# Staging the edge keys of a graph-layer count build on GpSimd instead of VectorE

## What is computed

```python
x = x + gnn(layernorm(x), stack([src, dst]), edge_attr, ...)
x = x + ffn(layernorm(x), ...)

def gnn(x, edge_index, edge_attr, ...):
    row, col = edge_index
    deg = segment_sum(ones, col);  dinv = where(deg > 0, deg ** -0.5, 0)
    norm = dinv[row] * dinv[col]
    for l in range(5):
        edge_fea = concatenate([edge_attr[:, 3:] @ ew1[l], edge_attr[:, 0:3] @ ew2[l]])
        msg = norm[:, None] * (h[row] + edge_fea)
        agg = segment_sum(msg, col)
        h = relu(concatenate([h, agg]) @ mlp_w[l] + mlp_b[l])
        h = batchnorm(h)            # relu too, but for the last layer
    return h
```

## Time and profile before

| | |
|---|---|
| median of three runs | 1666.47 us (1665.78 to 1670.65) |
| the profiled execution | 1666.33 us, its span 1664.6 us |
| TensorE (PE) busy | 1444.7 us, 87% |
| VectorE (DVE) busy | 705.1 us, 42% |
| ScalarE (ACT) busy | 389.3 us, 23% |
| GpSimd (POOL) busy | 165.3 us, 10% |
| one-hots cnt (L1521), x63 | 75.1 us, 1193 ns each |
| one-hots ohS (L1523), x504 | 117.6 us busy, 306 ns each |
| even and odd fields (L1625) | 93 and 61 instructions up to 440 us |

### The profile page before, as it was taken

One profiled execution on the slowest core, in us unless ns is written; L12 is line 12 of the kernel. 1 busy time (PEld: TensorE's weight loads), 2 busy tenths in 40 slices (PEclk: granted clock), 3 DMA queues, 4 the chain that ended last, 5 costly groups with the idle time before them and its releaser, 6 DMA issues.

```text
span 1664.6 us, 25197 instructions
## 1 busy us (share of the span) xinstructions
PE 1444.7 (87%) x8538; PEld 808.6 (49%) x8539; DVE 705.1 (42%) x1938; ACT 389.3 (23%) x1010; POOL 165.3 (10%) x145
## 2 busy tenths in 40 slices
PE   2565689889888999989999899989999863999996
PEld 2554444444443544445454444535444433666664
DVE  6989999999522220123001220122201356233332
ACT  1320444444302400032001310014000330333332
POOL 1000000000000000000000000000000004466663
PEclk9865799999999999989999999999999876999999
DMA  5153000000000000000000000000005090333333
GB/s 136 39 183 125 2 1 1 2 1 2 14 1 13 1 1 1 0 15 1 1 1 0 14 1 1 1 1 13 1 1 103 5 347 13 54 65 63 63 63 41
DMA packets 49551, 57.88 MB, mean 35 GB/s; under 512 B 14319, under 2 KB 41601, under 8 KB 49184
## 3 DMA queue, kind: packets, MB, share of 16 engines
q1 hardware_dynamic: 38688, 41.67, 8.7%
q0 software_dynamic: 10752, 14.69, 5.5%
HBM read 42.36 MB, written 13.99 MB: 34 GB/s over the span
## 4 chain that ended last, share of the span: by engine, by line
PE 79%; DVE 13%; issue 3%; DVEq 2%; ACT 1%; DMA 1%; POOL 1%; SPq 0%; POOLq 0%
PE bank L654 40%; PE bank L735 13%; PE bank L1148 6%; PE bank L1163 6%; PE bank L1752 3%; DVE ohS L1523 2%; PE bank L1697 2%; PE bank L1154 1%; PE bank L644 1%; DVE ohL L1409 1%; PE bank L738 1%; PE bank L1750 1%; PE bank L1140 1%; DVEq L505 1%; PE bank L1114 1%
## 5 line engine op out<-in xcount | busy, mean ns | idle before, releaser
L654 PE MATMUL bank<-at,m 125*128 125x500 fp8e4 (+1 forms) x3500 | 697.9, 356 | 10.4 <-issue 5.3
L654 PEld LDWEIGHTS bank<-at,m 125*128 125x128 f16 x3500 | 318.3, 98 | 342.8 <-issue 35.9
L663 DVE TENSOR_TENSOR aggT<-bank,dinvB 128x500 f32<-128x500 f32 (+1 forms) x70 | 42.3, 621 | 353.0 <-PE bank L654 352.8
L826 ACT ACTIVATE hT<-bank,prm 128x500 f32<-128x500 f32 (+1 forms) x70 | 40.5, 630 | 601.2 <-PE bank L738 601.2
L874 POOL TENSOR_TENSOR idJ<-idJ,wts 125x1400 f32<-125x1400 f32 x2 | 8.0, 4006 | 1380.6 <-DVE idJ L1032 1380.6
L788 DVE BATCH_NORM_STATS2 zst<-hT 128x6 f32<-128x500 f32 (+1 forms) x70 | 40.3, 617 | 198.4 <-ACT hT L826 198.4
L735 PE MATMUL bank<-hT,wcur 128*128 128x500 f32 (+1 forms) x280 | 124.2, 566 | 0.0
L1523 DVE TENSOR_SCALAR ohS<-iotaS,now 128x128 bf16<-128x128 bf16 x504 | 117.6, 306 | 0.0
L735 PE MATMUL bank<-aggT,wcur 128*128 128x500 f32 (+1 forms) x280 | 116.4, 538 | 0.0
L623 DVE SCALAR_TENSOR_TENSOR m<-bank,dinvP,m 125x256 f16<-125x256 f32 x100 | 48.0, 483 | 145.7 <-ACT m L635 145.7
L1148 PE MATMUL bank<-w1s,xtT 128*128 x224 | 107.7, 603 | 0.3 <-issue 0.2
(11 more groups left out here) (318 smaller groups left out, 1325.7 us busy)
## 6 DMA issues: line engine op xcount, KB each, us to landing
slrow<-sl_dram SPq DMA_DIRECT2D x26, 512.0 KB, 5.0
w1s<-in_L_ffn_W SPq DMA_DIRECT2D x1, 4096.0 KB, 14.5
w2s<-in_L_ffn_W SPq DMA_DIRECT2D x1, 4096.0 KB, 19.0
xin<-in_x SPq DMA_DIRECT2D x1, 2800.0 KB
x<-in_x SPq DMA_DIRECT2D x1, 2800.0 KB
out_rows<-x SPq DMA_DIRECT2D x1, 2800.0 KB
xn_dram<-xn SPq DMA_DIRECT2D x1, 2800.0 KB
wraw<-in_L_gnn_mlp_w SPq DMA_DIRECT2D x5, 512.0 KB, 3.7
```

Of the source, the lines that this page charges most:

```text
L654: last = pe.matmul(bank[banks[g % len(banks)]][:, 0:w], m[:, s, k, h * 128:(h + 1) * 128], at_block(g // H)[:, s, :], start=s == 0 and k = ...
```

## The change

GpSimd gets the staging of each strip (`stage`) and the odd fields (`high_nibbles`); VectorE keeps the one-hots and the even fields. GpSimd copies the keys first into a new buffer `rawKD` and waits for that copy (`s_raw`) before it subtracts the strip's offset. The odd fields are no longer shifted and masked: `encI - encB` leaves them four bits up, and ScalarE scales by 1/16 as it writes them. `s_nib` becomes `s_low` (VectorE) and `s_high` (GpSimd). The low nibbles, the one-hots and the order of VectorE's other steps stay.

```diff
+        def stage(pool, w):
+            side = w % 2
+            first, mine, past = first_chunk(pool, w), turns(pool, w), turns_before(pool, w)
+            with pool.Fori(0, mine) as i:
+                c = chunk_of(first, i)
+                pool.wait_ge(s_free[side], past + i + 1)
+                pool.tensor_copy(now[:, side, :, :], tab[:, :, bass.ds(c, U)])
+                pool.tensor_copy(rawKD[:, side, :, :], kd[:, :, bass.ds(c, U)]).then_inc(s_raw[side], 1)
+                pool.wait_ge(s_raw[side], past + i + 1)
+                pool.sem_inc(s_apart, 1)
+                pool.tensor_scalar(nowKD[:, side, :, :], rawKD[:, side, :, :], float(-W * w), None, ALU.add).then_inc(s_now[side], 1)
+
+        def high_nibbles(pool, u):
+            pool.wait_ge(s_low, u + 1)
+            pool.tensor_tensor(encI[:, u % 2, :], encI[:, u % 2, :], encB[:, :], ALU.subtract).then_inc(s_high, 1)
...
+            pool.wait_ge(s_rng, 1)
+            pool.wait_ge(s_ez, 1)
+            for w in range(NW):
+                stage(pool, w)
+                if w % 2 and w > 1:
+                    high_nibbles(pool, w // 2 - 1)
+            for u in range(PAIRS - 2, PAIRS):
+                high_nibbles(pool, u)
             gather_pool(pool)
...
-                dve.tensor_scalar(encB[:, :], encI[:, u % 2, :], NIBBLES, None, ALU.bitwise_and).then_inc(s_nib, 1)
-
-            def high_nibbles(u):
-                dve.wait_ge(s_nib, 2 * u + 1)
-                dve.tensor_scalar(encI[:, u % 2, :], encI[:, u % 2, :], 4, NIBBLES, ALU.logical_shift_right, ALU.bitwise_and).then_inc(s_nib, 1)
+                dve.tensor_scalar(encB[:, :], encI[:, u % 2, :], NIBBLES, None, ALU.bitwise_and).then_inc(s_low, 1)
...
-            ahead = first_chunk(dve, 0), turns(dve, 0), turns_before(dve, 0)
+            ahead = turns(dve, 0), turns_before(dve, 0)
...
                 with dve.Fori(0, mine) as i:
-                    c = chunk_of(first, i)
-                    dve.wait_ge(s_free[side], past + i + 1)
-                    dve.tensor_copy(now[:, side, :, :], tab[:, :, bass.ds(c, U)])
-                    dve.tensor_scalar(nowKD[:, side, :, :], kd[:, :, bass.ds(c, U)], float(-W * w), None, ALU.add).then_inc(s_now[side], 1)
                     dve.wait_ge(s_now[side], past + i + 1)
...
                 if side and w > 1:
                     low_nibbles(w // 2 - 1)
-                    high_nibbles(w // 2 - 1)
...
-                    act.wait_ge(s_nib, 2 * u + 1 + odd)
+                    act.wait_ge(s_high if odd else s_low, u + 1)
...
-                                              byte[:, f, :, 0:n], ACT.Copy, saturate=False,
+                                              byte[:, f, :, 0:n], ACT.Copy, scale=1.0 / 16 if odd else 1.0, saturate=False,
```

More of the change, by code:

```diff
@@ L147, in gnn_ffn_program @@
         nowKD = r("nowKD", [128, 2, 2, U], I16)
+        rawKD = r("rawKD", [128, 2, 2, U], I16)
         now = r("now", [128, 2, ROWS, U], BF16)
@@ L362, in gnn_ffn_program @@
         s_now = [sem(f"s_now{r}") for r in range(2)]
+        s_raw = [sem(f"s_raw{r}") for r in range(2)]
         s_oh = [sem(f"s_oh{r}") for r in range(2)]
@@ L366, in gnn_ffn_program @@
         s_enc = sem("s_enc")
-        s_nib = sem("s_nib")
+        s_low = sem("s_low")
+        s_high = sem("s_high")
         s_xf = sem("s_xf")
@@ L1509, in _ @@
             evicted = 0
-            ahead = first_chunk(dve, 0), turns(dve, 0), turns_before(dve, 0)
+            ahead = turns(dve, 0), turns_before(dve, 0)
             for w in range(NW):
                 side = w % 2
-                first, mine, past = ahead
+                mine, past = ahead
                 with dve.Fori(0, mine) as i:
-                    c = chunk_of(first, i)
-                    dve.wait_ge(s_free[side], past + i + 1)
-                    dve.tensor_copy(now[:, side, :, :], tab[:, :, bass.ds(c, U)])
-                    dve.tensor_scalar(nowKD[:, side, :, :], kd[:, :, bass.ds(c, U)], float(-W * w), None, ALU.add).then_inc(s_now[side], 1)
                     dve.wait_ge(s_now[side], past + i + 1)
@@ L1525, in _ @@
                 if w + 1 < NW:
-                    ahead = first_chunk(dve, w + 1), turns(dve, w + 1), turns_before(dve, w + 1)
+                    ahead = turns(dve, w + 1), turns_before(dve, w + 1)
                 if side and w > 1:
                     low_nibbles(w // 2 - 1)
-                    high_nibbles(w // 2 - 1)
                 if w > SB and w % SB == 3:
@@ L1539, in _ @@
                 low_nibbles(u)
-                high_nibbles(u)
             attribute_sums(NQ - 2)
```

## The result

The changed kernel takes 1709.32 us, the median of four runs (1707.82 to 1711.44), against 1667.43 us for the kernel before, measured beside it. The ratio is 1.025, with a 95% interval of 1.0228 to 1.0271: 2.5% slower. The forecast was 1716 us. The profiled execution took 1710.67 us, 44.3 more than the profiled one of before.

What follows compares the result with a forecast made beforehand. Count build paced by VectorE first, later by VectorE and TensorE nearly equally; turns 200.3, chains 99.6, gaps 12.8, evictions 4.8 sum to 317.5 us, last strip 49.3 us later; 1666.3 + 49.3 gives 1716 us, range 1683 to 1750.

Steps and rivals of the forecast that it cites:

- The sign: Whole kernel: slower than before, chance 0.92; same 0.05, faster 0.03.
- The chain, 2.88 us: From VectorE's low nibbles to the next ohD, after strips 3, 5, ... 61: VectorE waits 2.88 us for GpSimd's staging, 30 times.
- The subtraction hidden under the loads: GpSimd's 125x500 subtraction, about 0.9 us, lies beside 2.05 us of register loads and set-up, so costs nothing.
- the dearer rival: GpSimd's small operations stand behind long VectorE ones (19 us more), or the subtraction blocks register loads (27 more): 1735 to 1745 us; chance 0.15.
- The queue stands on its wait: GpSimd's queue does not run past an unmet wait, so three register loads, 1.65 us, come after it in each chain.
- the rival of 1684 us: GpSimd's queue runs ahead of its wait, register loads done meanwhile; chain 1.83 us, 31.5 us less; chance 0.17.
- 32 gaps of 0.40 us: At the other strip starts, GpSimd's copy and add exclude VectorE or wait for it: 0.40 us each, 12.8 us in all.
- The loop's end: What follows the count build loop needs the last dense groups as before and doesn't change; it shifts whole.
- The clock: Rival: TensorE idles more and runs at the lower clock; 0 to 8 us allowed, inside the range, no separate chance.
- TensorE covers it: Rival: from strip 13 on TensorE hides a chain of up to 1.25 us; about 1667 us; not slower or faster, chance 0.08.
- The rule on exclusion: Skill's statement that GpSimd and two-input VectorE operations exclude each other; the rows agree, the sum would be no other.

Runs made afterwards that it cites:

- e4: Changed kernel with GpSimd loading the next strip's three registers before it waits for the even fields; 1688.09 us, ratio 1.0107 to the kernel before.
- e1: Changed kernel with high_nibbles of a pair run after the staging of the next even strip instead of before it; 1670.73 us, ratio 1.0015 to the kernel before.
- e3: VectorE stages as in the kernel before, GpSimd does only the odd fields by the subtraction; 1673.41 us, ratio 1.0021 to the kernel before.
- e6: e3 with GpSimd's subtraction held until VectorE has done cnt of the next strip; 1673.69 us, ratio 1.0021 to the kernel before.
- e2: Changed kernel with only the staging on GpSimd, VectorE doing both nibbles by masks; 1663.18 us, ratio 0.9965 to the kernel before.

## Why the prediction was right, and where it was off

The sign, the mechanism and the place are as forecast: VectorE idles in front of ohD after each odd strip from 3 on and not after even ones, released by GpSimd, and everything behind the loop moves as a whole.

- *The chain, 2.88 us.* Measured 2.96 at 293.51. Its parts: loads and set-up from 290.60 to the copy at 292.61, 2.01 (forecast 2.05); copy 0.28 (0.28), behind whose first 0.22 us a second copy starts, rawKD, which the sum had forgotten; from its start to the add 0.40, and the add 0.25. The forecast of 0.25 + 0.15 for wait and add was too little, and the second copy was missing, but it had allowed up to 0.7 here. The mean over the 30 chains is 3.01 us, since in a few GpSimd's queue stood 0.3 us longer between two steps (3.30 us for the chain after strip 7); why, the record doesn't show. The attribute sums hid under the chain, as forecast. From first to last ohD the strips take 305.1 us; 62 turns of 3.18 and 8 evictions of 0.6 leave 103 us for the chains with their even fields, for which the sum had 99.6.
- *The subtraction hidden under the loads.* True: it ends at 291.89, the copy starts at 292.61. Its length was mis-sized, 1.25 instead of 0.9 us, inside the bound of 1.4, and it would have shown only from 2.05 on. e4 makes it visible. That it would keep the queue from loading registers, the other half of the dearer rival, is out as well: the first load starts at 290.60 and the subtraction at 290.64, side by side.
- *The queue stands on its wait.* This step carried the forecast against the rival of 1684 us. The 4.32 us without a queue operation, and the first load at 290.60, show it in this kernel, and in all 30 chains the first load starts 0.04 us before the subtraction; the trace has the wait on the subtraction itself, not on an instruction of its own; e4, which does by hand what the rival assumed, takes 1688 us. The measurement differs here from the Trainium skill (Perfetto Trace Analysis, Per-engine timelines), by which the sequencer is free again once the instruction is in the wait queue.
- *32 gaps of 0.40 us.* This is the term that failed: 12.8 us that aren't there. The gap after even strips is 0.00, but for one of 0.35 us between the second and third strip. The reasoning from the earlier trace rows took exclusion as a toll on each of GpSimd's operations. It is one, but it depends on what is met. GpSimd's small copies come 1.8 us into the turn, when VectorE is at its short ohS, and slip in; the longest ohS of the changed kernel took 0.41 us instead of 0.31, and the turn is 3.18 us all the same. With the chains, 3 us more than summed, that puts the last ohD at 473.2 instead of 482.3, 9 us early. The total is only 7 us under the forecast, since the part behind the loop, put at no change, got 4 us longer in the profiled execution: that much of the closeness is luck.
- *The loop's end.* The forecast called what follows the loop unchanged. About half a microsecond of the 4 is a second meeting with the subtraction. VectorE's multiplication in the last attribute sums, 0.17 us before, reads in the order of time:

```profile
482.19 1.24 POOL L539 TENSOR_TENSOR encI<-encI,encB 125x500 int32<-125x500 int32 x1 [4.04 <-DVE encB L1515]
...
482.26 1.20 DVE L1528 TENSOR_TENSOR s4P<-s4P,dinvP 125x16 f32<-125x16 f32 x1
```

  It happens in all six attribute sums that meet a subtraction. The 1.03 us is partly paid for by the odd fields that VectorE no longer does: from the last count products to the next dense product it is 8.15 us, 7.58 before.
- *The clock.* The forecast allowed 0 to 8 us. In the dense stretch the mean granted clock fell from 1.00 to 0.93, and between 168 us and the last count products TensorE was at its lower level, 1.2 GHz, for 72 us instead of 38. The ohD dates above add up without it, so inside the build it cost next to nothing: the 0.35 us gap, where GpSimd's copy waited for count products of 1.85 us. Behind the loop it was at the lower level for 124 us, 110 before. Over the traces of all eight kernels, that part goes from 1227 us with 110 us at the lower level to 1236 with 135. That fits the remaining 3.5 us; it was not isolated, and executions of one kernel differ by as much (1665.78 to 1670.65 before).
- *TensorE covers it.* The rival for no loss needed a chain of 1.25 us; it was 2.96. In e1, where the chain is all but gone, the pair is 7.9 us and the time that of before.
- *The rule on exclusion.* It was named beside the forecast as agreeing, and at this place the runs say more than the earlier trace rows could. e3 and e1 agree with the Trainium skill (SBUF — State Buffer, Who interferes with whom) for operations with two tensor inputs. e6 shows it for ohS, a `tensor_scalar`, which the same section counts among those that can contend.

## What to carry to other kernels

Before moving a step to an idle engine, write that engine's new program in order and find each place where a wait on the busy engine stands in front of something the busy engine needs next; double buffers don't help across it. Put the idle engine's register loads in front of its waits as well: three of them took 1.7 us here, and with the loop set-up they reached 0.77 us beyond the work beside them, 30 times: half of the loss. And count what the engines exclude each other from: GpSimd's small copies cost VectorE nothing beside short operations, but a 1.25 us operation cost it about 1 us at each of the places where the two were made to meet, more than twice the 0.43 us that it took off.

## What the runs showed of the hardware beyond that

- GpSimd took 1.25 us for the int32 subtraction of 125x500, 2.5 ns for each of the 500, where the undisturbed float32 product of the earlier trace rows took 1.8 for each of its 1400; a fixed cost in both is not separated. Its smallest operations took 0.20 (copy of 128x16) and 0.25 us (add on 128x16); VectorE did its two staging steps in 0.30.
- Of two operations that exclude each other, the one that started second waited, whichever engine it was: GpSimd's subtraction behind ohD (1.42 instead of 1.25 us, e1), cnt behind the subtraction (2.24 instead of 1.19, e1), GpSimd's copy behind cnt (1.14 instead of 0.28, e2). Between two back-to-back VectorE operations the waiting GpSimd operation got in: in e1 the subtraction, begun during ohD, ran before cnt.
